# New instruction orders on all five engines of a 64-tile attention kernel, and a separate written-out order for the end of the run

## The reference, cut to what matters

```
x = x + attn(modulated(x, cond))           # 16 heads of 64, two null keys, ALiBi bias, causal
x = x + ffn(cond2(x, cond))

modulated: y = clip((x * style) @ weight.T * demod + bias)
attn:  q = l2norm(layernorm(y) @ Wq); k, v = y @ Wkv; k = l2norm(k)
       softmax(q k^T * 8 + alibi, causal) @ v, then @ Wout
cond2: kx = modulated linear of x; softmax over heads of kx kx^T; times kx; modulated linear
ffn:   scores of 8 clusters and 64 tiles through a sigmoid and a piecewise linear table, two argmax,
       gather of the chosen tile's spline weights and direction, y = z + spline * direction, layernorm
```

## Time and profile before

| | |
|---|---|
| median of three runs | 1834.32 us |
| the profiled run | 1833.11 us |
| its span | 1831.3 us |
| PE busy | 1718.0 us, 94% |
| DVE busy | 1545.9 us, 84% |
| ACT busy | 1198.5 us, 65% |
| POOL busy | 1173.0 us, 64% |
| chain that ended last | PE 88%, DVE 5%, ACT 2% |

### The profile page before, as it was taken

The page is one execution under the profiler, slowest core; times in us unless marked ns, Lnnn a source line. Parts: engine busy times, 40 slices in busy tenths (PEclk is TensorE's granted clock), DMA queues, the critical chain, the costliest instruction groups (busy, mean ns, idle before and its releaser), DMA issues.

```text
span 1831.3 us, 62542 instructions
## 1 busy us (share of the span) xinstructions
PE 1718.0 (94%) x24806; PEld 1439.5 (79%) x24806; DVE 1545.9 (84%) x4182; ACT 1198.5 (65%) x2418; POOL 1173.0 (64%) x903
## 2 busy tenths in 40 slices
PE   4789999999999999999999999999999999999752
PEld 3568888888888888888888888888888888888641
DVE  5567799888989998889989988899899888998744
ACT  2456677777667777776676777676777777667431
POOL 0345557776777677767776777677767776776433
PEclk8899999999999999999999999999999999999875
DMA  4001222222222221222122212221222122212221
GB/s 150 15 9 29 42 49 49 49 55 59 48 46 53 59 49 45 53 59 49 45 56 56 52 42 55 56 52 45 55 54 55 43 52 55 55 47 50 55 54 44
DMA packets 341245, 93.63 MB, mean 51 GB/s; under 512 B 278289, under 2 KB 338097, under 8 KB 341169
## 3 DMA queue, kind: packets, MB, share of 16 engines
q1 hardware_dynamic: 338096, 82.04, 20.6%
q0 software_dynamic: 3072, 10.52, 2.1%
HBM read 58.95 MB, written 33.55 MB: 51 GB/s over the span
## 4 chain that ended last, share of the span: by engine, by line
PE 88%; DVE 5%; ACT 2%; POOL 1%; DMA 1%; issue 1%; SPq 1%; POOLq 0%; ACTq 0%; DVEq 0%
PE pa L442 29%; PE pb L421 7%; PE pa L449 6%; PE ps L645 6%; PE ps L487 6%; PE ps L472 5%; PE ps L479 4%; PE pc L542 4%; PE pc L622 3%; PE pa L421 3%; PE ps L557 3%; PE pb L433 3%; PE ps L489 2%; PE pb L551 2%; PE pb L428 2%; PE pc L568 1%
## 5 line engine op out<-in xcount | busy, mean ns | idle before, releaser
L1131 POOL TENSOR_TENSOR rn<-nrg,mhalf 128x16 f32<-128x16 f32 x64 | 186.6, 2915 | 160.6 <-DVE nrg L1037 160.6
L1117 POOL TENSOR_TENSOR rn<-nrg,mhalf 128x16 f32<-128x16 f32 x64 | 193.2, 3018 | 119.5 <-DVE nrg L970 119.4
L442 PE MATMUL pa<-wv,y 128*128 128x512 f32 x768 | 209.6, 409 | 0.0
L442 PE MATMUL pa<-wq,xnTs 128*128 128x512 f32 x768 | 205.1, 411 | 0.3 <-ACT kcat L703 0.3
L442 PE MATMUL pa<-wk,y 128*128 128x512 f32 x768 | 194.3, 402 | 0.9 <-ACT qn L722 0.9
L442 PEld LDWEIGHTS pa<-wq,xnTs 128*128 128x128 f32 x768 | 139.3, 191 | 51.8 <-issue 23.5
L442 PEld LDWEIGHTS pa<-wk,y 128*128 128x128 f32 x768 | 139.3, 188 | 30.9 <-ACT qn L722 1.7
L1111 POOL TENSOR_TENSOR pr<-pr,rden 128x1056 f32<-128x1056 f32 x64 | 124.7, 1949 | 54.5 <-DVE rden L943 51.8
L442 PEld LDWEIGHTS pa<-wv,y 128*128 128x128 f32 x768 | 135.4, 189 | 23.2
L1006 DVE TENSOR_TENSOR qn<-qn,rn 128x1024 f32<-128x1024 f32 x64 | 112.7, 1762 | 15.6 <-POOL rn L1117 15.0
L1092 POOL TENSOR_TENSOR kn<-kn,rn 128x1024 f32<-128x1024 f32 x64 | 122.0, 1905 | 5.0
(11 more groups left out here) (216 smaller groups left out, 4863.3 us busy)
## 6 DMA issues: line engine op xcount, KB each, us to landing
xT<-in_xT SPq DMA_DIRECT2D x64, 128.0 KB
x<-in_x SPq DMA_DIRECT2D x64, 128.0 KB, 2.1
kxdr<-kxn SPq DMA_DIRECT2D x64, 128.0 KB, 1.7
x1d<-x SPq DMA_DIRECT2D x64, 128.0 KB, 1.8
vm<-kxdr SPq DMA_DIRECT2D x128, 64.0 KB
odr<-o SPq DMA_DIRECT2D x256, 32.0 KB
on<-odr SPq DMA_DIRECT2D x64, 128.0 KB
xb<-x1d SPq DMA_DIRECT2D x64, 128.0 KB, 2.2
```

Source lines behind the costliest of these rows:

```text
L442: last = mm(bank, part(lhs(a_, k)), part(rhs(b_, k)), start=(n == 0), stop=(n == 3 * CK - 1))
L1117: g.tensor_tensor(rn[:, 0, :], nrg[:, 0, :], mhalf[:, :], ALU.pow).then_inc(S("q_rsqrt"), 1)
L1131: g.tensor_tensor(rn[:, 1, :], nrg[:, 1, :], mhalf[:, :], ALU.pow).then_inc(S("k_rsqrt"), 1)
```

## The change

No operation is added to a tile or removed from one. Four things change.

First, `pipeline` takes a second function, `tail`, and runs it behind the loop in place of the unrolled steps 62 to 74. Each engine has its own tail, a list of calls and waits with constants, in an order that is no longer that of `step`. Second, the body of `step` is cut into 108 small functions `do_...(t, p)`, so that both can call them. Third, `step` has a new order on each engine, and other distances between stages: q and k are projected in step t + 1 (before t + 2), v, the transposes and the scores in t + 2, the weighted sum in t + 3, the residual in t + 4, the second attention in t + 5, its output linear in t + 6, the routing in t + 7, the gather in t + 8, the spline in t + 9, the output in t + 10, and its DMA in t + 12. Fourth, waits follow the new order; two of them are new in kind: POOL's spread waits for the second attention's weighted sum of the tile before (`av_mm`), since it stands earlier in the step, and PE waits for the residual by a semaphore of its own (`x1_done`). `pause` becomes two columns wide.

```diff
-        def pipeline(eng, step):
+        def pipeline(eng, step, tail):
...
-            for i in range(last, T + 11):
-                step(i, i % 2)
+            tail()
...
+            def do_spread(t, p):
+
+                g.tensor_tensor(vbd, bc(vm[:, p, :], 1, QG), bc(pick4[:, :], 2, G * DM), ALU.mult)\
+                    .then_inc(S("spread"), 1)
...
+                if live(i, 5):
+                    if live(i, 6):
+                        wait(pool, "av_mm", t6)
+                    wait_dma(pool, "v2_in", t5, 1 - p, 2)
+                    do_spread(t5, 1 - p)
+                if live(i, 2):
+                    wait(pool, "q_guard", t2)
+                    do_qpow(t2, p)
...
+            def tail():
+
+                pe.wait_ge(D("v2_in", 1), 928)
+                pe.wait_ge(S("o2_done"), 57)
+                do_kT(57, 1)
+                pe.wait_ge(S("k0_raw"), 61)
+                do_v0(60, 0)
...
-            pipeline(pe, step)
+            pipeline(pe, step, tail)
```

More of the change, by code:

```diff
@@ new lines, in do_kxn, with do_kT0, do_pv, do_sTt @@
+            def do_kxn(t, p):
+                from_T(two(pb, 0), kxT).then_inc(S("kxn_mm"), 1)
+            def do_kT0(t, p):
+                four(pa[:, 0, :], kn, 0).then_inc(S("kT0_mm"), 1)
+            def do_pv(t, p):
+                for r in range(HP):
+                    for t, s in ((0, 0), (1, 1), (1, 0), (0, 1)):
+                        last = pv_tile(r, t, s, p)
+                last.then_inc(S("pv_mm"), 1)
+            def do_sTt(t, p):
+                for q in range(QG):
+                    last = nc.tensor.transpose(pc[:, q * P:(q + 1) * P], sT[:, q, :], ident[:, :])
+                last.then_inc(S("mix_s"), 1)
@@ new lines, in do_simA, with do_zns, do_xnT @@
+            def do_simA(t, p):
+                for r, t, s in HEADS:
+                    last = sim_tile(r, t, s)
+                last.then_inc(S("sim_shared"), 1)
+            def do_zns(t, p):
+                from_T(two(pb, 0), zT)
+                for k in range(CK):
+                    last = mm(pb[:, C:C + NS + CH], zT[:, k, :], wsc[:, k, :],
+                              start=(k == 0), stop=(k == CK - 1), skip_group_check=True)
+                last.then_inc(S("score_mm"), 1)
+            def do_xnT(t, p):
+                to_T(two(pa[:, 2, :], 0), xn).then_inc(S("xnT_mm"), 1)
@@ new lines, in do_xnTe, with do_rk0, do_exp @@
+            def do_xnTe(t, p):
+                for k in range(CK):
+                    last = fn(xnT[:, k, :], pa[:, 2, k * P:(k + 1) * P], ACT.Identity,
+                              bias=cols[:, NBI, k:k + 1], scale=cols[:, NG, k:k + 1])
+                last.then_inc(S("xnT_done"), 1)
+            def do_rk0(t, p):
+                fn(sq[:, 0 * 512:1 * 512], pa[:, 0, :], ACT.Square)
+                fn(kn[:, 0 * 512:1 * 512], pa[:, 0, :], ACT.Copy).then_inc(S("k0_raw"), 1)
+            def do_exp(t, p):
+                fn(pr[:, :, :, :], pr[:, :, :, :], ACT.Exp).then_inc(S("probs"), 1)
@@ new lines, in do_rk1, with do_xnTh, do_gelu, do_mask @@
+            def do_rk1(t, p):
+                fn(sq[:, 1 * 512:2 * 512], pa[:, 1, :], ACT.Square)
+                fn(kn[:, 1 * 512:2 * 512], pa[:, 1, :], ACT.Copy).then_inc(S("k1_raw"), 1)
+            def do_xnTh(t, p):
+                fn(part(xnTs[:, p, 0, :, :]), xnT[:, :, :], ACT.Copy).then_inc(S("xnT_high"), 1)
+            def do_gelu(t, p):
+                if p == 1:
+                    fn(hT[:, :], pb[:, C:C + P], ACT.Gelu, bias=b1[:, :]).then_inc(S("gelu_done"), 2)
+            def do_mask(t, p):
+                for g in range(QG):
+                    last = fn(kbd[:, g, :], pc[:, 0:2 * P], ACT.Identity, bias=0.0, scale=pick4[:, g:g + 1])
+                last.then_inc(S("mask_done"), 1)
@@ L792, in _ @@
+            pipeline(act, step, tail)
         @block.vector
@@ new lines, in do_yTa @@
+            def do_yTa(t, p):
+                modulate(yT, two(pa[:, 2, :], 0), dem[:, 0, :, :], t).then_inc(S("y_dem"), 1)
+                wait(dve, "y_dem", t)
+                for k in range(CK):
+                    last = v.tensor_scalar(yT[:, k, :, :], yT[:, k, :, :], cols[:, CB, k:k + 1], CLAMP, ALU.add, ALU.min)
+                last.then_inc(S("y_min"), 1)
+                wait(dve, "y_min", t)
+                v.tensor_scalar(part(y3[:, p, 0, :, 0:BT, :]), yT[:, :, :, :], -CLAMP, None, ALU.max)
+                v.tensor_scalar(part(y3[:, p, 0, :, BT, :]), yT[:, :, 0, :], -CLAMP, None, ALU.max)\
+                    .then_inc(S("y_high"), 1)
+                wait(dve, "y_high", t)
+                v.tensor_scalar(yT[:, :, :, :], yT[:, :, :, :], -CLAMP, None, ALU.max).then_inc(S("yT_done"), 1)
```

2379 lines of the change are left out of this document (1879 added, 500 removed).

## The result

The changed kernel takes 1854.0 us (median of four runs, 1848.85 to 1855.4) where the kernel before takes 1834.13: a ratio of 1.0103, 95% interval 1.0088 to 1.0119. It is slower by 1%, and the forecast of 1790 us, with a range up to 1834, is missed on the other side. The profiled run is one of 1854.13 us with a span of 1852.3.

The account below looks back on a forecast made before the run. PE was taken to bound the kernel (94% busy, saturated in the loop), VectorE close behind. The span 1831.3 - 7 (loop) - 6 (fill) - 30 (drain) = 1788.3, + 1.8 + 1.2 = 1791, stated as 1790 us; range 1768 to 1834.

Parts of the forecast that it names:

- The loop: The 57 or so saturated steps between fill and drain: step from 26.11 to 26.0 us, -7 us in all.
- list of holds: VectorE held by GpSimd in the new step: routing chain 0.7, k's guard 0.55, yT's copy 1.14 us.
- the prediction's own sign: In the loop: wrong in kind if it moves by more than 0.3 us a step either way.
- bound "+3": Slow end of the loop's term of -7 us: a step 0.05 us over the old one.
- VectorE becomes the bound: Rival: one more held VectorE instruction in each loop step, +0.6 us a step, +34, so 1824 us; chance 0.16.
- The first: Rival: GpSimd's spread starts before VectorE's guard of q, +1.6 us a step, +91, 1879 us; chance 0.17.
- 12.3 us of the earlier trace: In the loop: PE's weight load idle 0.20 us a tile over 62 tiles, read as waiting for VectorE's bias.
- The fill: First steps: -6 us, bounds -11 and 0, mainly from fewer waits of y's transpose for yT's copy.
- 10.7: Us of PE work moved ahead of the last k projection, taken off the drain's gain of 40.8.
- The drain: Last k projection to the end: pieces sum to 105.7 against 146.5 us; gain taken as -30.
- the prediction's signs: For the drain: near 116 instead of 146.5 us, last tile's x1 transpose within 28 us of its scores.
- the second piece: In the drain, last tile's scores to the transpose of x1: 25 us taken where 39.4 was.

Follow-up runs that it names:

- e6_yl_before_own: Changed kernel with VectorE's low-part subtractions of y (do_yTl) one place earlier in the loop's step, behind do_oh and ahead of do_own: 1794.33 us.
- e4_guard_late: Changed kernel with, in the loop's step, do_yTl behind do_share and VectorE's moments of y (do_mom) ahead of q's norm, delaying q's guard: 1897.1 us.
- e3_end_by_steps: Changed kernel with the written-out end left out; the loop's step function runs on for steps 62 to 75: 1860.75 us.
- e2_gather_alone: Changed kernel with GpSimd's xb and gamma behind ve in the loop's step, so that nothing behind the gather can start at once: 1802.39 us.

## Why the prediction was wrong

**The loop is the step that failed, and in it the list of holds.** "In the new order I find three such places of known length": all three are in the trace, each smaller in the loop than I had it: the guard of k lasts 0.57 in the mean where 0.17 is its own (a hold of 0.40, not 0.55), the routing chain's L1960 0.84 where 0.29 is its own (0.55, not 0.7), the two instructions of L2020 0.63 each for 0.28 (0.7, not 1.14). The fourth was missing. The prediction does not name this pair. By the rule it works with, that an instruction holds from its start, a subtraction that ends ahead of `xb` is free; behind a gather the rule failed, and it cost 1.83 us a step. Without it (e6_yl_before_own) the step is 25.96, inside the 25.85 to 26.0 forecast. Of the 1.83 freed, L2055 takes up 0.48, and PE, busy for 999.90 of 1000 us, sets the step before the rest is used, so the two steps differ by 1.13 us. Against the step of 26.0 that was forecast, 57 x 1.09 = 62 us are nearly all of the 64 us between forecast and time. By the prediction's own sign (a loop that moves by more than 0.3 us a step) it was wrong in kind.

The loop of before could not have shown it: there DVE ran a reduction, which the gather did not lengthen, beside it. The drain of before had a hint:

```profile
1765.35 0.76 DVE L963 TENSOR_TENSOR zT<-zd,cols 128x256 f32<-128x256 f32 x1
```

```profile
1764.76 1.03 POOL L1106 DMA_INDIRECT gs<-in_gath,row  x1 [0.16 <-issue]
1765.81 0.87 POOL L1114 TENSOR_TENSOR yn<-yn,gb 128x256 f32<-128x256 f32 x1
```

`zT`, 0.42 us where nothing holds it, would have ended at 1765.77, ahead of the record of the instruction behind the gather, and took 0.76; 33 us later the same happens once more. It is not the same hold, since it ends inside L1114, which is itself lengthened (0.73 elsewhere), but it says that the recorded start is not the bound. The bound "+3" for the loop had no room for a hold outside the list, and that is what made the range wrong too.

**The rivals.** The second, "VectorE becomes the bound", is what happened, by one more hold as described; its price was mis-sized: +0.6 a step over the forecast of 26.0, from a hold of 0.7 to 1.9 less the room; the hold was 1.83 and the step 1.09 over. It had a chance of 0.16 and a time of 1824. The first did not happen. e4_guard_late shows its price, but the distance on which it hangs was wrong for the change: the guard leads there by 0.32 to 0.35 us from 430 us on (0.19 to 0.28 in e6_yl_before_own), not by 0.0 to 0.16:

```profile
1035.14 0.17 DVE L1927 TENSOR_SCALAR nrg<-nrm 128x16 f32<-128x16 f32 x1
```

```profile
1035.47 1.90 POOL L2555 TENSOR_TENSOR bd<-vm,pick 128x1024 f32<-128x1024 f32 x1 [4.81 <-PE pc L813]
```

**The loop's gain.** Even freed, the step is 25.96 where 26.11 was; the sum of PE's groups, 25.85, was 0.1 too low. -7 would have been -5 at this mark (1516.0 to 1511.3 from tile 5's k to the last). The prediction read the 12.3 us of the earlier trace rows as a wait for VectorE's bias; the row names PE's own score products (L472), and the kernel makes PE's next group wait until the first sixty are over. The size was right all the same: in the change this wait is 0.9 us in four.

**The fill.** Taken at -6; tile 5's k starts 3.0 later in the change and 0.7 later in e6_yl_before_own. But by this mark PE has done more: it has been busy for 132.37 us (1423 products) in the change and 133.12 (1423) in e6_yl_before_own, and for 124.17 (1121) before. This is the work that moved forward, which the prediction had taken off the drain (10.7). Without these 8 to 9 us the fill is ahead by some 5 and 8 us, an estimate from these numbers, so -6 was about right. By whole waits the account was right too; the rows of the changed kernel, the answers to the earlier trace rows, are

```profile
PE pa L612 <- ACT kn L1365: 5.6, 2, 3.8
...
PE pa L603 <- DVE yT L2027: 3.7, 2, 1.8
```

Two of six waits for yT's copy stay, 3.7 of 9.4 us, and the new ones for k's squares are 5.6 us in two (1.6 and 4 expected).

**The drain.** Forecast 105.7 us from the last k to the end by the sum of its pieces (the prediction's signs say 116 for the same stretch, which does not fit that sum), measured 110.7. The milestones that answer to the earlier trace rows:

```profile
1758.66 1.55 PE L642 MATMUL ps<-kcat,qp 64*64 64x66 f32 x64
...
1788.89 0.44 PE L598 MATMUL pb<-ident,x 128*128 128x128 f32 x2
...
1837.51 0.99 POOL L2587 DMA_INDIRECT gs<-in_gath,row  x1
```

The pieces are 17.1 (18 forecast), 30.2 (25), 48.6 (48) and 14.8 (14.7). The size was right but for the second piece, scores to the transpose of x1, 5 us too small and over the 28 us of its sign; the cause was partly not. I put it down to the order in which other groups stand between; e3_end_by_steps shows that all but about 8 us come with the step's new distances and order.

**The sum.** Freed of the one hold, the kernel takes 1794.3 us where 1790 was forecast. That it comes so near is partly luck: at the marks of the table, with the 10.7 counted in the fill, where it lands, the forecast is +4.7, -7 and -40.8, and e6_yl_before_own has +0.7, -4.7 and -35.8, so a better fill pays for half of what the loop and the drain lack. Two sums are off by 2 us: 1790 + 91 is 1881, not 1879, and the low end with -15, -9 and -40 is 1770, not 1768; neither changes the outcome. The conclusion was wrong by its sign, for the one hold.

## What to carry to other kernels

When an order is packed until a second engine has little room left in a step, one held instruction decides the sign: give a range that has room for a hold that the rows of the loop don't show, above all where two engines come to meet in pairs that they did not meet in before. Look at the busy time of the engine that gained no work: 125 us more for the same instructions pointed to holds at once, and the instruction whose mean grew most (0.28 to 2.11) named the place. Then move that one instruction, not the plan: one place earlier was worth 60 us here.

## What the runs showed of the hardware

An elementwise GpSimd instruction that stands directly behind a gather (an indirect DMA) held VectorE before its own record begins: a two-operand subtraction that would have ended 0.23 us ahead of that start waited for its end, 1.42 us for 0.28, with `xb` and with `gamma` alike; the gather with nothing behind it that could start left the subtraction at 0.28. The written-out end of the change has a wider case: `own` (0.22 us), begun 0.60 us behind a gather, would have been over 0.5 us ahead of the record of the spread behind it, and took 2.73, to the spread's end. Whether the instruction takes hold early or its record starts late, the traces do not tell, and the `zT` of before, lengthened to 0.76 only, shows that the hold is not always to the end. With two of them in a row the subtraction waited for both, 2.11. Why it did not get in between is open, since in e2_gather_alone DVE's L2088 did get in between the same two instructions in every second step (0.60 us), and gamma took 0.91 there in place of 0.74.

The gather is not without effect itself: in e6_yl_before_own the normalisation of y, a `tensor_scalar` from SBUF to SBUF, starts 0.35 us behind the gather, takes 0.89 for 0.41 and ends 0.18 us after the gather's record, 0.6 ahead of the end of the `xb` behind it. Where it starts 0.28 us behind a gather, in the written-out end of the change, it takes its 0.41, and the gather 1.30 for 1.07. In no run does this instruction begin inside a gather with nothing queued behind it. The Trainium skill ("SBUF — State Buffer", section "Who interferes with whom") states that a copy or `tensor_scalar` can take both ports of the shared pair, while a `tensor_tensor` takes its read side only; a gather that needed the write side alone would give both rows, though no run here separates the sides.

As to who goes first, the measured distances are close: the spread won with a lead of 0.04 us, the guard with one of 0.05. And not every GpSimd instruction holds: inside the power of k's guard (2.91 us from 1018.01 in the change) VectorE's `xnTs`, begun at 1018.27, took 0.41, no more than L2060 of the same size (0.42).
